# Experts of a mixture-of-experts layer: the weights become TensorE's stationary operand, the tokens the moving one, in tiles of two halves

## The reference

```python
NUM_EXPERTS = 12; TOP_K = 2; FFN_DIM = 320; HIDDEN = 512
logits = x @ gate_w.T
top_w, top_i = jax.lax.top_k(softmax(logits), TOP_K)
top_w = top_w / jnp.sum(top_w, axis=-1, keepdims=True)
for e in range(NUM_EXPERTS):
    h = jax.nn.silu(x @ w1[e].T) * (x @ w3[e].T)      # 512 -> 320, twice
    out = out + h @ w2[e].T * cw[:, e:e + 1]          # 320 -> 512
```

## Time and profile before

| what | us |
|---|---|
| median of three runs | 752.61 |
| lowest and highest of them | 751.52 and 754.05 |
| the profiled execution's own time | 752.36 |
| its span (first to last instruction) | 750.5 |
| PE busy in it | 713.3 |

### The profile page before, as it was taken

One profiled execution on the slowest core, in us unless ns is written; L12 is line 12 of the kernel. 1 busy time (PEld: TensorE's weight loads), 2 busy tenths in 40 slices (PEclk: granted clock), 3 DMA queues, 4 the chain that ended last, 5 costly groups with the idle time before them and its releaser, 6 DMA issues. The chain is left out here.

```text
span 750.5 us, 17847 instructions
## 1 busy us (share of the span) xinstructions
PE 713.3 (95%) x6231; PEld 518.5 (69%) x6232; DVE 499.4 (67%) x1102; ACT 341.9 (46%) x695; POOL 304.7 (41%) x336
## 2 busy tenths in 40 slices
PE   9999899999999999999999988999999999999994
PEld 4777677787877778687765877666666666666641
DVE  3857968879788797795968886444444444444477
ACT  3866654656556566586475202222222222222264
POOL 0574465563654645545511002244434444344210
PEclk9999999999999999999999999999999999999998
DMA  8824365354652545536310026455465555522955
GB/s 322 317 76 149 126 221 174 98 171 129 200 188 88 176 139 169 183 131 222 113 72 15 30 106 221 166 196 209 155 216 219 208 208 201 205 84 87 336 237 194
DMA packets 40124, 126.78 MB, mean 169 GB/s; under 512 B 4224, under 2 KB 4608, under 8 KB 38144
## 3 DMA queue, kind: packets, MB, share of 16 engines
q1 hardware_dynamic: 31024, 99.49, 38.2%
q0 software_dynamic: 6880, 22.55, 9.0%
q10 hardware_dynamic: 2160, 3.93, 1.4%
HBM read 81.13 MB, written 44.83 MB: 168 GB/s over the span
## 5 line engine op out<-in xcount | busy, mean ns | idle before, releaser
L1088 DVE COPY_PREDICATED ST<-msk,pS 128x256 f32<-128x256 uint8 x224 | 121.2, 570 | 50.8 <-issue 23.8
L763 POOL TENSOR_TENSOR piece_parts<-piece,piece_parts 128x1024 f16<-128x1024 f32 x48 | 104.1, 2170 | 99.7 <-ACT piece_parts L708 99.7
L1582 PE MATMUL pH<-ring,xgh 128*128 x344 | 103.0, 299 | 4.1 <-DVE xgl L1787 2.1
L1583 PE MATMUL pH<-ring,xgh 128*128 x344 | 102.9, 299 | 0.0
L1584 PE MATMUL pH<-ring,xgl 128*128 x344 | 102.9, 299 | 0.0
L757 POOL TENSOR_TENSOR RL<-RL,AM 128x256 f32<-128x256 f32 x96 | 72.1, 751 | 73.7 <-ACT RL L700 67.8
L1893 POOL DMA_INDIRECT y_scratch<-ysb,sidx x43 | 42.7, 993 | 128.9 <-DVE ysb L1798 126.1
L401 PE MATMUL pS<-RL 64*128 64x64 f32 (+2 forms) x1536 | 89.1, 265 | 0.0
L401 PEld LDWEIGHTS pS<-RL 64*128 64x128 f32 (+1 forms) x1536 | 84.4, 178 | 2.2
L1782 DVE TENSOR_TENSOR hid<-pH,sil 128x320 f32<-128x320 f32 x43 | 21.1, 492 | 95.4 <-issue 48.7
L741 DVE TENSOR_TENSOR RL<-RL,AM 128x256 f32<-128x256 f32 x96 | 70.4, 734 | 14.5 <-ACT RL L687 12.7
(11 more groups left out here) (254 smaller groups left out, 1533.2 us busy)
## 6 DMA issues: line engine op xcount, KB each, us to landing
piece<-in_w_experts SPq DMA_DIRECT2D x48, 512.0 KB, 5.0
w_split_scratch<-piece_parts SPq DMA_DIRECT2D x48, 512.0 KB, 3.8
ring<-w_split_scratch SPq DMA_DIRECT2D x12, 2048.0 KB
yin<-y_scratch SPq DMA_DIRECT2D x16, 512.0 KB, 13.0
out_x<-X SPq DMA_DIRECT2D x8, 512.0 KB, 2.8
x_scratch<-X ACTq DMA_DIRECT2D x15, 256.0 KB, 2.0
X<-in_x SPq DMA_DIRECT2D x2, 1536.0 KB, 17.7
RL<-in_wxT SPq DMA_DIRECT2D x4, 256.0 KB, 5.1
```

The source lines that it names most:

```text
L763: g.tensor_tensor(piece_parts[buf][:, 1, :], piece[buf][:, :], piece_parts[buf][:, 0, :], ALU.subtract).then_inc(piece_lo, 1)
L1088: v.copy_predicated(out[:, :, :, 0 if lv == 0 else 1, :], msk[:, lv, :, :].rearrange(shape, m=m), pS[:, :, lv * S:(lv + 1) * S].rearrange( ...
L1582: pe.matmul(p[:, 0, 0:F], xgh[par][:, k, :], wh, start=(k == 0), stop=False)
L1583: pe.matmul(p[:, 0, 0:F], xgh[par][:, k, :], wl, start=False, stop=False)
```

## The change

The tiles still hold 128 pairs, but in two halves of 64, each half with an expert of its own. An expert's pairs are filled up to a multiple of 64, so 76 halves (`HALVES`), that is 38 tiles (`SLOTS`), are enough.

In a matmul the weights are now stationary and the tokens of one half (64 columns) are moving. `hidden(i, par, half)` makes five blocks of 128 rows (w1 and w3 have 320 rows each, 640 = 5 x 128), each from four chunks of features by three terms: 60 matmuls for a half. Its output already has features on partitions, so `turn_hidden` is gone. `down` has, for each half, four blocks of outputs by eight matmuls, 64 in a tile. Its output has features on partitions too, so ACT copies it (`copy_turned`) and PE turns it back with four transposes (`turn_out`). SiLU, gate and the splitting go by halves.

```diff
-SLOTS = (NT * 2 * P + E * (P - 1)) // P
+HALVES = (NT * 2 * P + E * (S - 1) + E) // S
+SLOTS = (HALVES + 1) // 2
+HALVES = 2 * SLOTS
+BLOCKS = 5
...
-                v.tensor_tensor(oh_tile[:, at, :], slot_h[:, :].rearrange("p (o n) -> p o n", o=1).broadcast_to([P, NT, SLOTS]),
-                                tile_h[:, at].rearrange("p (n o) -> p n o", o=1).broadcast_to([P, NT, SLOTS]), ALU.is_equal).then_inc(tile_ready, 1)
+                v.tensor_tensor(oh_tile[:, at, :], slot_h[:, :].rearrange("p (o n) -> p o n", o=1).broadcast_to([P, NT, HALVES]),
+                                tile_h[:, at].rearrange("p (n o) -> p n o", o=1).broadcast_to([P, NT, HALVES]), ALU.is_equal).then_inc(tile_ready, 1)
...
-                need, slot = [nc.values_load(tabi[0:1, k, bass.ds(i, 1)], engines=PE, min_val=lo, max_val=hi,
-                                             skip_runtime_bounds_check_because="an expert's number or place")
-                              for k, lo, hi in ((0, 1, E), (1, 0, RING - 1))]
+                tok = slice(half * S, (half + 1) * S)
+                need, slot = table(0, i * 2 + half), table(1, i * 2 + half)
...
                 pe.wait_ge(w_ready, need)
-                for n, p in ((0, pH1), (1, pH3)):
+                for b in range(BLOCKS):
+                    o = pH[half][:, 0, b * S:(b + 1) * S]
                     for k in range(KT):
-                        at = k * 2 * F + n * F
-                        wh, wl = weights(slot, P, at, F)
-                        pe.matmul(p[:, 0, 0:F], xgh[par][:, k, :], wh, start=(k == 0), stop=False)
-                        pe.matmul(p[:, 0, 0:F], xgh[par][:, k, :], wl, start=False, stop=False)
-                        t = pe.matmul(p[:, 0, 0:F], xgl[par][:, k, :], wh, start=False, stop=(k == KT - 1))
+                        wh, wl = weights(slot, k * 2 * F + b * P)
+                        pe.matmul(o, wh, xgh[par][:, k, tok], start=(k == 0), stop=False)
+                        pe.matmul(o, wl, xgh[par][:, k, tok], start=False, stop=False)
+                        t = pe.matmul(o, wh, xgl[par][:, k, tok], start=False, stop=(k == KT - 1))
                 t.then_inc(h_full, 1)
...
-            def turn_hidden(i):
-                pe.wait_ge(hid_out, i + 2)
-                for k in range(FT):
-                    t = pe.transpose(pHT[:, 0, k * P:(k + 1) * P], hid[:, k * P:(k + 1) * P], idt[:, :])
-                t.then_inc(ht_full, 1)
-
-            def down(i, slot):
-                pe.wait_ge(ht_out, i + 1)
-                for k in range(FT):
-                    wh, wl = weights(slot, P, KT * 2 * F + k * C, C)
-                    pe.matmul(pO[:, 0, :], hTh[:, k, :], wh, start=(k == 0), stop=False)
-                    t = pe.matmul(pO[:, 0, :], hTh[:, k, :], wl, start=False, stop=(k == FT - 1))
-                    if k < FT - 1:
-                        pe.matmul(pO[:, 0, :], hTl[:, k, :], wh, start=False, stop=False)
+            def down(i, par):
+                for half in range(2):
+                    slot = table(1, i * 2 + half)
+                    pe.wait_ge(ht_out, i * 2 + (half + 1))
+                    for c in range(KT):
+                        o = pY[:, 0, c * P + half * S:c * P + (half + 1) * S]
+                        for k in range(FT):
+                            wh, wl = weights(slot, KT * 2 * F + k * C + c * P)
+                            pe.matmul(o, wh, hTh[par][:, k, half, :], start=(k == 0), stop=False)
+                            if k < FT - 1:
+                                pe.matmul(o, wh, hTl[par][:, k, half, :], start=False, stop=False)
+                            t = pe.matmul(o, wl, hTh[par][:, k, half, :], start=False, stop=(k == FT - 1))
                 t.then_inc(o_full, 1)
+            def turn_out(i):
+                pe.wait_ge(y_copied, i + 1)
+                pe.wait_ge(o_out, i + 1)
+                for c in range(KT):
+                    t = pe.transpose(pO[:, 0, c * P:(c + 1) * P], yT[:, c, :], idt[:, :])
+                t.then_inc(y_full, 1)
...
-            def tile(i, k, rounds=None):
-                down(i - 1, hidden(i, k % 2, i - 1))
+            def tile(i, k, rounds=None, former=True):
+                hidden(i, k % 2, 0)
                 if rounds is not None:
                     turn(i + 2, k + 2, rounds)
-                turn_hidden(i)
+                if former:
+                    turn_out(i - 2)
+                down(i - 1, (k + 1) % 2)
+                hidden(i, k % 2, 1)
```

More of the change, by code:

```diff
@@ new lines, in table, with hidden @@
+            def table(k, h):
+                lo, hi, why = ((1, E, "an expert's number, plus 1"), (0, RING - 1, "a place in the ring"))[k]
+                return nc.values_load(tabi[0:1, k, bass.ds(h, 1)], engines=PE, min_val=lo, max_val=hi,
+                                      skip_runtime_bounds_check_because=why)
+            def hidden(i, par, half):
+                tok = slice(half * S, (half + 1) * S)
+                need, slot = table(0, i * 2 + half), table(1, i * 2 + half)
+                if half == 0:
+                    pe.wait_ge(xt_out, i + 2)
+                    if not isinstance(i, int) or i:
+                        pe.wait_ge(hid_out, i * 2 - 1)
+                pe.wait_ge(w_ready, need)
+                for b in range(BLOCKS):
+                    o = pH[half][:, 0, b * S:(b + 1) * S]
+                    for k in range(KT):
+                        wh, wl = weights(slot, k * 2 * F + b * P)
+                        pe.matmul(o, wh, xgh[par][:, k, tok], start=(k == 0), stop=False)
+                        pe.matmul(o, wl, xgh[par][:, k, tok], start=False, stop=False)
+                        t = pe.matmul(o, wh, xgl[par][:, k, tok], start=False, stop=(k == KT - 1))
+                t.then_inc(h_full, 1)
@@ L1653, in high_x, with silu, high_hidden, copy_turned @@
                 a.copy(xgh[par][:, :, :], pXT[par][:, 0, :].rearrange("p (k t) -> p k t", k=KT)).then_inc(xg_hi, 1)
[L1655 to L1667 removed]
+            def silu(h, half):
+                a.wait_ge(h_full, h + 1)
+                u = pH[half][:, 0, 0:BLOCKS * S].rearrange("p (b t) -> p b t", t=S)
+                a.activation(sil[:, half, 0:2, :], u[:, 0:2, :], ACT.Silu)
+                a.activation(sil[S:P, half, 2, :], u[0:S, 2, :], ACT.Silu).then_inc(sil_out, 1)
+            def high_hidden(h, par, half):
+                a.wait_ge(hid_out, h + 1)
+                a.copy(hTh[par][:, :, half, :], hid[:, half, :, :]).then_inc(ht_hi, 1)
+            def copy_turned(i):
+                a.wait_ge(o_full, i + 2)
+                a.copy(yT[:, :, :], pY[:, 0, :].rearrange("p (c t) -> p c t", c=KT)).then_inc(y_copied, 1)
+            def first_half(i, par):
+                silu(i * 2, 0)
+                high_hidden(i * 2, par, 0)
+            def tile(i, par, more=True, next=True):
+                silu(i * 2 + 1, 1)
+                if more:
+                    high_x(i + 2, par)
+                high_hidden(i * 2 + 1, par, 1)
+                if next:
+                    first_half(i + 1, 1 - par)
+                copy_turned(i)
             high_x(0, 0)
@@ L1672, in _ @@
             a.activation(ptop[:, :, :], ptop[:, :, :], ACT.Exp).then_inc(exp_done, 1)
-            tile(0, 0)
-            tile(1, 1)
+            first_half(0, 0)
             pairs = (SLOTS - 2) // 2
-            with a.Fori(1, pairs) as j:
+            with a.Fori(0, pairs) as j:
                 tile(j * 2, 0)
@@ L1679, in _ @@
             for i in range(pairs * 2, SLOTS):
-                tile(i, i % 2, more=i + 2 < SLOTS)
+                tile(i, i % 2, more=i + 2 < SLOTS, next=i + 1 < SLOTS)
             a.wait_ge(wtop_ready, 1)
@@ L1827, in _ @@
             for i in range(pairs * 2, SLOTS):
-                tile(i, (i - 1) // 2, i % 2, more=i + 2 < SLOTS)
+                tile(i, (i - 1) // 2, i % 2, more=i + 2 < SLOTS, next=i + 1 < SLOTS)
             copy_out(SLOTS - 1, (SLOTS - 1) // 2, (SLOTS - 1) % 2)
@@ L1899, in _ @@
             g.sem_inc(g_waited, 1)
[L1900 removed]
+            g.wait_ge(list_ready, 2)
             g.sem_inc(g_waited, 1)
```

177 lines of the change are left out of this document (87 added, 90 removed).

## The result

The changed kernel takes 1293.75 us (median of four runs, 1290.82 to 1295.93), the kernel before 753.11 (four runs, 751.52 to 754.05): 1.718 times as long, interval 1.713 to 1.723. The forecast was 1244 us with a range of 1140 to 1340. The profiled execution took 1294.2 us, its span is 1292.3.

The account below looks back on a forecast made before the run. PE was taken as bound by its array before, by its sequencer's register instructions after. 752.4 - 254.2 (old stage) + 733 (38 tiles of 19.3) + 10 + 2 + 1 = 1244 us, range 1140 to 1340.

Parts of the forecast that it names:

- The first rival: Register instructions hide beside the array, so the array bounds at 6.2 us a tile: 737 us, chance 0.04.
- The second: Each matmul costs a fixed 62 ns to issue, register instructions beside it: 953 to 1079 us, chance 0.05 (anything between 760 and 1140).
- Array: PE's 184 short matmuls at 0.029 us plus 8 transposes: 6.2 us a tile, alone gaining some 18 us.
- Sequencer: PE's 128 register instructions a tile at 0.125 us each: 16.0 us, no longer hidden by 6.2 us of array work.
- Reads of the table: On PE, 6 table reads a tile instead of 3, with waits, register instructions and branch: 3.3 us a tile.
- Bounds: Distance per register instruction on PE between 0.105 us (636 us for 38 tiles) and 0.15 us (855 us).
- the third rival: Register distances of 0.15 us and more, or late instruction blocks throughout (64 us more): 1340 us and above, chance 0.09.
- Instructions: PE's loop body does not stay in the queue; a block is waited for at 8 jumps back: 10 us.
- Entry, 2 us, and exit, 1 us: Larger one-hot builds on DVE and table chain before the stage; a copy and four transposes after the last tile.
- Clock: PE may fall to 1.2 GHz, still hidden behind the sequencer; exit up to +9 us, none taken.
- Signs: If right: four tiles in 77 us, PE's busy share a third to half, register instructions 0.125 us apart.
- Other engines: Extra DVE, ACT and POOL work, ring loads and scatters cost nothing, covered by 19.3 us a tile.

Follow-up runs that it names:

- constant-place kernels: Changed kernel reading weights from fixed ring place 0, no register instructions: 857.1 us; 758.86 with gathers ahead of scatters; 745.41 also without table reads.
- the seventh kernel: Changed kernel with weights from constant ring place 0, gathers ahead of scatters on POOL and no table reads on PE: 745.41 us, ratio 0.990.

## Why the prediction was right

The mechanism was right: PE's sequencer is the bound, at two register instructions for each group of three short matmuls. Taking them away brings the matmuls to 0.03 us, adding them to the kernel before makes that one slow. The first rival, that they hide, fails by a factor of five (0.1325 against 0.026). The second, a fixed price of 62 ns a matmul, fails in the constant-place kernels, 0.029. That rests on thousands of matmuls, where the earlier trace rows had 32.

The sum came out 50 us short. By its terms:

- *Array, 6.2 us a tile.* Measured 6.3, where nothing else is in the way. But the 18 us that this was to gain over the stage before were 8 there (245.8 us against 254.1).
- *Sequencer, 128 x 0.125 = 16.0 us.* Mis-sized: 0.1325, so 17.0. Over 38 tiles that is 37 us, most of the error. The earlier trace rows show two rows of eight starts, rounded to 0.1 us: 15 distances in 1.8 to 2.0 us, 0.12 to 0.133 and not 0.12 to 0.13. Fifteen distances hold at most two of the longer ones. A sum that multiplies by 4864 wants a longer sample. The 43 tiles of the kernel before would have given 0.128 (845 distances, 59 of them 0.15 or longer), which is worth 16 of these 37 us; that the longer ones come more often in the new stream, only the new trace shows.
- *Reads of the table, 3.3 us a tile.* 20.3 - 17.0 = 3.3, by difference. Right.
- *Bounds.* 0.105 and 0.15 held it. The 0.20 of the earlier trace rows was not, as I took it, a case at the start of a stretch, but one of those 59 longer distances. And late blocks, priced in the third rival at 64 us more, would give 1308 us, inside the range and not "1340 us and above".
- *Instructions, 10 us.* Mis-sized: seven stops of 3.4 us, 24. That the body does not stay was right, that one block of 0.9 us is all that is waited for was not, and the sign "gaps of microseconds behind L1636" that I had given to the third rival came. Inside the body no stops appear, so that part of the third rival did not come.
- *Tiles outside the loop* have constant indices and no such register instructions. I had not seen this saving. The 136 of them and the 120 ALU_OP in the 32 tiles of the loop are 0.8 us a tile, 4.8 for the six tiles outside; what the stage lacks against the terms above is 4.
- *Entry, 2 us, and exit, 1 us.* The first matmul of a tile comes at 467.3 us, not 463.3: 4. In the profiles of the other kernels with this entry it comes between 462.9 and 469.9, so these 4 us are within the scatter. The exit is 1292.3 - 1257.5 = 34.8 against 33.0: 2.
- *Clock.* It fell to the lower level for most of the stage and cost nothing there, as forecast: the mean distance of register instructions is 0.132 at either level. In the whole exit the clock is 0.84 against 0.89, and the up to 9 us that it might have cost did not come: the seventh kernel, at 0.89 there, has an exit of 34.5 us too.
- *Signs.* Four tiles take 84.6 us, where I had 77. And I had wanted PE's busy share in the stage to fall to a third or half. It is 0.86 (677.81 of 790.20), from 0.98: a duration of 0.23 us covers the distance to the next matmul, so the busy share does not show an idle array.
- *Other engines, nothing.* Right for this kernel, and wrong in the words "if the sequencer cost were gone, they would have 6.2 us of cover, still enough on DVE's sum". A sum of busy time says nothing about an order. POOL's gather behind its scatter cost 95 us as soon as the sequencer was out of the way.

Together: 37 + 14 - 4 + 2 + 1 = 50 us.

The page's rule that a jump to a block not held stalls (the Trainium skill, "Runtime: NRT & Kernel Launch", section "Instruction fetch mechanics") is borne out by the 3.4 us at L1636. Its room of 2048 instructions for PE is not. I counted PE's instructions between two branches in each trace:

| kernel | instructions in the body | branch, median us |
|---|---|---|
| before | 429 | 0.22 |
| before, 64 columns | 1453 | 0.22 |
| constant place, no reads | 1564 | 0.21 |
| constant place | 1577 | 0.21 |
| constant block in `hidden` | 1785 | 3.67 |
| changed kernel | 2115 | 3.41 |

In the loops of the four bodies up to 1577, the queue of instructions brings at most one block while they run round; in the two others it brings all of them again. The point from which it stops lies between 1577 and 1785 here. By the page's 2048, the body of 1785 should have jumped freely.

One reading to beware of: the view of waits puts 16.8 us ahead of L1588 down to DVE's `hid` (L1817). In PE's stream that wait stands on the register instruction ahead of the first matmul (L1588), behind the one for the ring (L1583). Their rows tell another story:

```profile
L1583 PEldq EVENT_SEMAPHORE  x38: 51/51/51, 467.1 to 1230.0; - x38
L1588 PEldq FUSED_REGOPS  x1520: 46/46/46, 467.3 to 1248.4; - x190
```

Both take the same time every time, and from the start of L1583 to that of L1588 behind it are 0.105 to 0.111 us in all 38 tiles. Nothing was waited for; the idle time is the table reads and the address ahead of the first matmul.

What stays open: why about every eighth distance is longer. It is so in the loop and without it, so it is not the jump. In the changed kernel two longer ones follow each other most often (273 of 551 times) by exactly 32 of PE's instructions; which mechanism it is, no run here tells.

## What to carry to other kernels

Count what the sequencer must do per matmul, not only columns: a register address cost 0.13 us here each time it was set, so it was free ahead of 320 columns (0.136 us each, two addresses for three matmuls) and cost its whole price ahead of 64. Before cutting matmuls shorter, make their addresses constant, or leave them long. And when one bound is removed, read the order on the queues behind it, since their busy sums do not show who stands behind whom.

## What the hardware showed that I had not expected

- A weight load of 128 x 128 fp16 for every 64-column matmul, over thousands of them in the constant-place kernels, is no burden: 0.029 us each at 2.4 GHz, 0.053 at 1.2 GHz.
- A jump of PE's loop costs 0.2 us up to a body of 1577 instructions and 3.4 to 3.7 in the median at 1785 and 2115, up to 6.1.
- The mean distance of register instructions is the same at both levels of TensorE's clock, 0.132 us.
